# New order lists for the five engines of a four-layer graph network kernel, drawn up with two more costs counted

## The reference, cut to what matters

```python
x = _layernorm(x + _L0(x, adj))   # two hypergraph convolutions: H = (adj != 0), relu and a norm between them
x = _layernorm(x + _L1(x, adj))   # one softmax weight per node: softmax(q . (adj @ k)) times v
x = _layernorm(x + _L2(x, adj))   # attention, 8 heads of 32, scores times 2*adj, softmax, output projection
x = _layernorm(x + _L3(x, adj))   # gate from the degree, sigmoid scores times adj, divided by their sum, relu
```

## Time and profile before

| what | us |
|---|---|
| runs of the kernel, median (lowest to highest) | 962.69 (962.51 to 967.75) |
| profiled execution, span from first to last instruction | 966.0 |
| TensorE busy in the span | 887.1 (92%) |
| VectorE, ScalarE, GpSimd busy | 742.3, 724.6, 670.3 |
| steady part, from 194.1 to 857 | 662.9 |

### The profile page before, as it was taken

The page is one execution under the profiler, slowest core; times in us unless marked ns, Lnnn a source line. Parts: engine busy times, 40 slices in busy tenths (PEclk is TensorE's granted clock), DMA queues, the critical chain, the costliest instruction groups (busy, mean ns, idle before and its releaser), DMA issues.

```text
span 966.0 us, 34322 instructions
## 1 busy us (share of the span) xinstructions
PE 887.1 (92%) x12124; PEld 761.5 (79%) x12124; DVE 742.3 (77%) x2292; ACT 724.6 (75%) x1740; POOL 670.3 (69%) x1005
## 2 busy tenths in 40 slices
PE   4778898999999999999999999999999999988674
PEld 3556677888888888888888888888888888876542
DVE  5556776888888888888888888888888888876632
ACT  3445567888888888888888888888888888867631
POOL 2575667777777787777777777877778777764421
PEclk9798899999999999999999999999999999999955
DMA  8002443444454444444344444443443444444320
GB/s 207 20 21 83 111 100 65 119 111 106 112 123 121 116 116 102 103 112 109 106 109 110 122 123 117 114 106 99 111 119 103 104 115 116 109 97 116 97 48 22
DMA packets 194573, 99.46 MB, mean 103 GB/s; under 512 B 112866, under 2 KB 194276, under 8 KB 194532
## 3 DMA queue, kind: packets, MB, share of 16 engines
q1 hardware_dynamic: 194532, 98.93, 40.6%
HBM read 48.28 MB, written 25.17 MB: 76 GB/s over the span
## 4 chain that ended last, share of the span: by engine, by line
PE 53%; ACT 11%; POOL 10%; DVE 10%; issue 9%; DMA 5%; SPq 1%; POOLq 0%; DVEq 0%; ACTq 0%
PE bank L537 12%; PE bank L539 12%; PE bank L538 12%; POOL rFl L1375 3%; PE bank L562 3%; ACT r L886 3%; PE bank L754 2%; PE bank L815 2%; DMA k_by_head<-kst 2%; DMA Ks<-k_by_head 2%; PE bank L650 1%; ACT x L846 1%; PE bank L682 1%; ACT rFh L826 1%; POOL rsC L1391 1%
## 5 line engine op out<-in xcount | busy, mean ns | idle before, releaser
L1375 POOL TENSOR_TENSOR rFl<-r,rFh 128x512 f16<-128x512 f32 x64 | 74.2, 1160 | 81.1 <-ACT rFh L826 81.1
L537 PE MATMUL bank<-z1h,W 128*128 128x256 f16 x256 | 71.9, 281 | 6.3 <-DVE z1l L1025 6.3
L538 PE MATMUL bank<-z1l,W 128*128 128x256 f16 x256 | 71.8, 281 | 0.0
L537 PE MATMUL bank<-W,rFh 128*128 128x256 f16 x256 | 71.8, 280 | 0.0
L539 PE MATMUL bank<-z1h,W 128*128 128x256 f16 x256 | 71.7, 280 | 0.0
L539 PE MATMUL bank<-W,rFl 128*128 128x256 f16 x256 | 71.7, 280 | 0.0
L538 PE MATMUL bank<-W,rFh 128*128 128x256 f16 x256 | 71.7, 280 | 0.0
L1476 POOL TENSOR_TENSOR late<-late,Smx 128x512 f32<-128x512 f32 x64 | 66.8, 1043 | 1.3 <-DVE Smx L1282 1.0
L1375 POOL TENSOR_TENSOR y0l<-y,y0h 128x512 f16<-128x512 f32 x32 | 37.3, 1166 | 42.3 <-ACT y0h L826 42.3
L870 ACT ACTIVATE Pf<-bank,Dinv 128x128 f32<-128x128 f32 x64 | 20.0, 363 | 49.7 <-DVE Dinv L1167 49.7
L886 ACT ACTIVATE r<-bank,b1c 128x256 f32<-128x256 f32 x128 | 50.1, 471 | 4.8 <-PE bank L539 4.8
(11 more groups left out here) (281 smaller groups left out, 4188.3 us busy)
## 6 DMA issues: line engine op xcount, KB each, us to landing
Qs<-q_by_head SPq DMA_DIRECT2D x96, 128.0 KB, 2.7
Ks<-k_by_head SPq DMA_DIRECT2D x96, 128.0 KB, 3.2
Vbd<-vst SPq DMA_DIRECT2D x128, 66.0 KB, 2.1
xin<-x SPq DMA_DIRECT2D x32, 256.0 KB, 2.8
q_by_head<-qst SPq DMA_DIRECT2D x32, 256.0 KB, 2.5
k_by_head<-kst SPq DMA_DIRECT2D x32, 256.0 KB, 2.1
out<-late SPq DMA_DIRECT2D x32, 256.0 KB, 2.9
aC<-adj_mask SPq DMA_DIRECT2D x32, 65.0 KB, 2.2
```

The costliest lines, as they stand in the source:

```text
L537: pe.matmul(o, sh, mh, start=start, stop=False, skip_group_check=True)
L538: pe.matmul(o, sh, ml, start=False, stop=False, skip_group_check=True)
L1375: return pool.tensor_tensor(dst, a, b, ALU.subtract)
```

## The change

All lists of the five engines are replaced, apart from a few that come out the same; the pieces themselves, the waits and the buffers stay. The lists of before were drawn up in the same form; for the new ones two more costs are counted: what TensorE loses where the kind of matmul changes (part of the array or all of it), and that VectorE and GpSimd keep each other waiting at a port that they share. Two lines of the diff:

```diff
-ORDER_PE = [3, 2, 1, 5, 2, 4, 4, 2, 0, 3, 1, 0, 2, 0, 5, 4, 0, 0, 5, 3, 1, 3, 4, 5, 1, 2, 5, 5, 2, 0, 1, 0, 4]
+ORDER_PE = [3, 2, 1, 3, 2, 5, 0, 2, 1, 4, 4, 5, 0, 2, 0, 4, 1, 3, 3, 5, 0, 0, 5, 4, 1, 2, 5, 5, 1, 2, 0, 0, 4]
-ORDER_POOL = [0, 1, 0, 0, 1, 0, 3, 4, 1, 1, 1, 2, 1, 2, 0, 5, 3, 0, 0, 0, 4, 4, 3, 4, 5, 5, 5, 0, 0]
+ORDER_POOL = [1, 0, 0, 0, 1, 4, 0, 1, 1, 1, 3, 2, 1, 2, 5, 3, 0, 0, 0, 4, 4, 0, 3, 4, 5, 5, 5, 0, 0]
```

More of the change, by code:

```diff
@@ L61 @@
-TAIL_POOL = [[1, 1, 3, 4, 5, 1, 1, 1, 3, 1, 2, 2, 3, 4, 4, 4, 5, 5, 5], [4, 3, 5, 2, 2, 4, 4, 3, 3, 4, 5, 5, 5], [4, 5, 4, 4, 3, 4, 3, 5, 3, 5, 5], [4, 5, 4, 4, 4, 5, 5, 5], [5, 5, 5, 5]]
+ORDER_PE = [3, 2, 1, 3, 2, 5, 0, 2, 1, 4, 4, 5, 0, 2, 0, 4, 1, 3, 3, 5, 0, 0, 5, 4, 1, 2, 5, 5, 1, 2, 0, 0, 4]
+ORDER_SP = [3, 0, 3, 4, 3, 0, 0, 2, 3, 3, 5, 2, 2]
+HEAD_SP = [[0, 0, 0], [0, 0, 0], [0, 0, 2, 0, 2, 2], [3, 3, 3, 0, 0, 2, 3, 3, 0, 2, 2], [3, 3, 4, 0, 0, 3, 0, 2, 3, 3, 2, 2], [3, 4, 0, 3, 3, 0, 2, 3, 0, 3, 2, 2, 5]]
@@ new lines @@
+TAIL_SP = [[3, 4, 3, 3, 3, 5, 2, 3, 2, 2], [3, 3, 5, 3, 4, 3, 2, 3, 2, 2], [3, 4, 3, 3, 5, 3, 3], [5, 4], [5]]
+ORDER_ACT = [0, 3, 1, 4, 2, 3, 5, 0, 5, 0, 5, 1, 0, 2, 4, 4, 1, 4, 2, 0, 0, 5, 0, 0, 0, 0, 2, 1, 4, 3, 3, 4, 2, 3, 3, 4, 5]
+ORDER_DVE = [0, 0, 2, 0, 0, 2, 1, 0, 0, 3, 0, 3, 0, 0, 2, 1, 1, 4, 1, 4, 4, 2, 3, 4, 0, 5, 2, 5, 0, 3, 5, 5, 4, 1, 5, 3, 3, 5, 4, 2, 1, 5, 3, 5, 1, 1, 5, 2, 3, 3, 0, 0, 4, 0]
+ORDER_POOL = [1, 0, 0, 0, 1, 4, 0, 1, 1, 1, 3, 2, 1, 2, 5, 3, 0, 0, 0, 4, 4, 0, 3, 4, 5, 5, 5, 0, 0]
@@ new lines @@
+HEAD_PE = [[0, 0, 0, 0, 0, 6, 6, 6, 0, 0], [1, 0, 0, 0, 1, 0, 0, 1, 1, 0, 1, 0], [2, 1, 2, 0, 2, 0, 2, 0, 1, 0, 0, 2, 6, 1, 2, 1, 0, 1, 0], [3, 2, 1, 2, 3, 2, 1, 0, 2, 0, 3, 0, 3, 1, 0, 2, 0, 1, 2, 1, 0, 0], [1, 3, 2, 4, 4, 0, 3, 1, 0, 4, 2, 2, 0, 2, 4, 0, 3, 1, 0, 3, 2, 4, 1, 2, 1, 0, 0], [2, 1, 3, 5, 3, 2, 1, 0, 4, 4, 2, 5, 2, 0, 4, 5, 3, 0, 3, 4, 5, 0, 0, 1, 5, 2, 5, 1, 2, 1, 0, 0, 4]]
+HEAD_ACT = [[6, 0, 0, 0, 0, 0, 0, 0, 0, 0, 0, 6], [0, 6, 0, 0, 1, 0, 0, 0, 0, 1, 0, 0, 1, 0, 1], [6, 2, 0, 6, 0, 0, 1, 0, 2, 2, 0, 0, 2, 0, 1, 0, 0, 1, 0, 2, 1], [6, 6, 6, 6, 0, 3, 2, 6, 1, 3, 0, 0, 2, 1, 0, 1, 2, 3, 2, 0, 0, 0, 0, 0, 0, 2, 1, 6, 3, 3, 3], [4, 1, 3, 0, 0, 0, 2, 3, 4, 4, 0, 4, 1, 2, 4, 0, 2, 4, 0, 0, 1, 0, 0, 2, 0, 1, 4, 3, 2, 3, 3, 3], [0, 3, 1, 5, 5, 2, 4, 3, 5, 0, 0, 4, 2, 4, 0, 4, 2, 5, 1, 4, 0, 0, 0, 1, 0, 0, 2, 0, 3, 1, 3, 4, 2, 3, 3, 4, 5]]
@@ new lines @@
+HEAD_POOL = [[0, 0, 0, 6, 6, 0, 0, 0, 0, 0, 0, 0], [0, 0, 6, 0, 0, 1, 1, 1, 1, 1, 6, 1, 0, 0, 0, 0, 0, 0], [0, 0, 0, 0, 1, 1, 2, 2, 6, 1, 1, 1, 0, 0, 0, 0, 1, 0, 0], [0, 0, 1, 0, 0, 1, 3, 1, 1, 1, 2, 1, 3, 2, 3, 0, 0, 0, 0, 0, 0], [1, 0, 0, 0, 1, 3, 0, 4, 1, 1, 1, 1, 2, 2, 4, 4, 3, 4, 0, 0, 0, 0, 3, 0, 0], [1, 0, 1, 0, 0, 4, 3, 0, 1, 1, 2, 2, 5, 1, 3, 4, 1, 4, 0, 0, 0, 0, 3, 4, 5, 5, 5, 0, 0]]
+TAIL_PE = [[2, 1, 3, 5, 3, 2, 1, 2, 4, 4, 5, 2, 4, 5, 3, 3, 4, 5, 1, 2, 5, 5, 1, 2, 4, 1], [3, 3, 5, 4, 2, 4, 5, 4, 2, 2, 5, 2, 5, 3, 3, 4, 2, 5, 5, 2, 4], [3, 3, 5, 4, 4, 4, 5, 4, 5, 3, 3, 5, 5, 5, 4], [5, 4, 4, 5, 4, 5, 4, 5, 5, 5, 4], [5, 5, 5, 5, 5, 5]]
@@ new lines @@
+TAIL_ACT = [[3, 1, 2, 3, 5, 4, 5, 5, 4, 4, 2, 1, 2, 5, 4, 1, 2, 4, 3, 3, 4, 1, 3, 2, 3, 4, 5], [3, 4, 3, 5, 5, 5, 2, 4, 4, 4, 5, 2, 2, 3, 2, 4, 3, 4, 2, 3, 3, 4, 5], [3, 3, 5, 5, 4, 4, 4, 5, 4, 4, 5, 4, 3, 3, 3, 3, 4, 5], [5, 4, 5, 5, 4, 4, 4, 5, 4, 4, 4, 5], [5, 5, 5, 5, 5]]
+TAIL_DVE = [[2, 1, 3, 2, 1, 2, 1, 4, 2, 4, 3, 4, 5, 4, 3, 5, 1, 2, 5, 4, 5, 3, 5, 3, 3, 5, 3, 4, 1, 2, 5, 3, 5, 1, 5, 2, 3, 1, 4, 1], [3, 4, 2, 3, 4, 4, 4, 5, 2, 5, 2, 2, 5, 5, 5, 2, 3, 4, 5, 3, 3, 3, 4, 3, 2, 5, 3, 5, 5, 2, 3, 4], [3, 3, 4, 4, 4, 4, 4, 5, 3, 5, 4, 5, 5, 5, 3, 3, 5, 3, 3, 3, 5, 5, 3, 5, 4], [4, 4, 4, 4, 5, 5, 4, 5, 5, 5, 4, 5, 5, 5, 5, 4], [5, 5, 5, 5, 5, 5, 5, 5, 5]]
@@ L63 @@
+TAIL_POOL = [[1, 1, 3, 4, 1, 1, 1, 2, 2, 5, 1, 3, 3, 4, 4, 4, 5, 5, 5], [4, 3, 5, 2, 2, 3, 3, 4, 4, 4, 5, 5, 5], [3, 4, 5, 4, 4, 3, 3, 4, 5, 5, 5], [4, 5, 4, 4, 4, 5, 5, 5], [5, 5, 5, 5]]
 LAST_LAG = 5
```

9 lines of the change are left out of this document (1 added, 8 removed).

## The result

The changed kernel takes 971.03 us (median of 20 runs, 965.33 to 981.45), the kernel before 962.60 us in the same rounds: a ratio of 1.0089, 95% interval 1.0065 to 1.0113. It is slower by 0.9%, inside the band of 1% that was called the same and inside the range, and 7.6 us above the predicted 963.4.

What follows compares the result with a forecast made beforehand. TensorE was taken to bound the steady steps, chains of waits the head and tail. +0.20 us a step over 26 steps (+5.2) and -4.5 in the tail gave 963.4 us; range 955 to 972, over all cases 948 to 977.

Steps and rivals of the forecast that it cites:

- The turn of x1: Steady step: TensorE would newly wait about 0.7 us for normB in each step, bounds 0.2 and 0.9.
- Rival A: Faster: nbB misses Ql or VectorE's short ops are quicker, x1's turn waits only 0.2; -0.30 a step, 950.4 us; chance 0.27.
- Changes of kind: TensorE's steady step: ten changes between part and whole array become six, 0.35 us less a step, bounds 0.27 and 0.60.
- SAs: Steady step: TensorE's wait at the turn of SAs falls from 0.32 to some 0.15 us, 0.15 less a step.
- rival B: Slower: step's end becomes VectorE's, resb holds HBh, TensorE waits at L608 for HBl; +0.70 a step, 976.4 us; chance 0.23.
- the step's +0.20: Net steady-step forecast in us: -0.35 kinds, -0.15 SAs' wait, +0.70 x1's turn; 26 times, +5.2.
- the 26.6 to 26.8: Sign of a right forecast: steady steps of this length in us; below 26.3 or above 27 would show it wrong.
- SyncE: Keys' way through DRAM: starts earlier, covering the scores' moving forward; 0 taken, a failed cover joining the wait at x1's turn.
- the 0.7: The forecast wait in us of TensorE at the turn of x1 in each steady step.
- Tail: Context fills a gap in the last step but one, about 1.5 us earlier; three tail steps give -4.5, bounds 0 and 9.
- Head: No gain expected in the head: 0 us, bounds -4 and +4, a tenth of its idle time.

## Why the prediction was right, and where it was not

- **The turn of x1.** +0.70 forecast, 0.70 measured, on normB as said, with nbB beside Ql. That the size is met to the hundredth is luck: two terms were too large by 0.4 each. The turn came 3.2 nearer to L614, not 3.6, since conv2's wait and the turn of P's stand in front of it. The chain to normB's end became 1.0 shorter, not 1.4: from L614 to mvB's end are 3.30 where 3.1 was the most, preB starting only behind conv2, and the pair took 1.05 where 0.94 was put in. Rival A, whose point was that nbB misses Ql, fell with that.
- **Changes of kind.** -0.35 forecast, -0.25 measured: the term was mis-sized. o1 and uxT, which differ in rows only, cost 0.11 between them, twice what I kept for it. The rule of the Trainium skill's TensorEngine Tiling (Array Packing), section Tiling Modes, that every change of mode drains the engine, agrees with that row, and its sum (0.30) was the nearer one.
- **SAs.** -0.15 forecast, -0.21 measured.
- **What failed: rival B put in the wrong place.** I named its cause (GpSimd and VectorE late at the end of the step) but priced it only where it would hold HBh and TensorE would wait at L608, and set it aside because VectorE had 0.99 of cover there. So the sum has no term for it. The cover was used up: the low part of k, 0.87, moved into it, and y0 waits 0.30 for rsc. B's own meeting came as well, resb beside HBh, and HBh's two ops took 0.63 instead of 0.41; TensorE does not wait at L608 for it. What cost time came out at conv2, which waits 0.31 a step for y0l; the change had brought conv2 1.1 nearer to L608 (v's 1.34 out from between, the sum L696 in). And rvar was not the late one; the cause is the place of El0 and El1 beside veG and rsG, which I had read only as a delay for rvar, and which makes GpSimd reach y0l late. With it, and with 0.1 less for the kinds, the step's +0.20 becomes +0.6, 16.6 us where 5.2 stood: 27.12, and not the 26.6 to 26.8 that was to show the forecast right.
- **SyncE.** "If that cover fails, the wait joins the 0.7 rather than adding to it": the run with Ql moved shows that: the scores wait for Ks, 0.20 on the mean, once the turn hardly waits.
- **Tail.** -4.5 forecast, 5.7 in the profile. TensorE idles 3 to 4 us less in the tail; the rest goes with the clock. In the last step but one, the place that was priced, the context fills the gap (its second half waits 0.87 for its own input), the second projection no longer waits (the 0.93 of the earlier trace rows), and the turn of cx follows it at once:

```profile
932.67 0.87 PE L754 MATMUL bank<-Vbd,PT 128*64 128x66 f16 x24
934.41 0.57 PE L754 MATMUL bank<-Vbd,PT 128*64 128x66 f16 x24 [0.87 <-DMA PT<-Ehl]
934.92 0.28 PE L537 MATMUL bank<-Wl,xgFh 128*128 128x256 f16 x1
...
936.24 0.60 PE L562 MATMUL bank<-ident,late 128*128 128x128 f32 x4
937.81 0.22 PE L792 MATMUL bank<-Qh 128*64 128x64 f16 x2 [0.97 <-DVE y3l L1025]
```

  From the first projection to the turn of cx are 6.0 us instead of 9.2. TensorE idles 0.9 of them instead of 2.2, which is close to the forecast 1.5; the rest is the clock, 0.72 in this stretch instead of 0.50. Behind the turn s3 then waits 0.97 for y3l.

- **Head.** 0 forecast, with 4 as bound, and 5.1 came in the profile. But TensorE's idle time in the head is 40.2 us before, 39.8 and 40.2 in the two executions with the new ends and the old steady lists, and 38.1 in the changed kernel. So the waits gave 0 to 2, inside the bound, and the rest is busy time, at a clock of 0.94 to 0.95 instead of 0.92. Over the 13 profiles with these head lists the head ends between 160.9 and 166.6; of before there is one profile, with 167.3.
- **The sum.** By the profiles the steady steps missed by 9.5 us (14.7 where 5.2 stood), and the head by 5.1 and the tail by 1.2 the other way; these offset each other in part, and the forecast's place inside 1% owes something to that.

## What to carry to other kernels

In a list where several chains end together, shortening one of them alone gains little: each edit that moved one op out of the way of a wait in the changed step met another wait, of 0.2 to 0.8 us, within the same microsecond. So before moving an instruction read who waits for everything that it passes, not only for what it heads, and what else the op that it heads waits for: 0.69 us taken out in front of preB brought mvB forward by 0.01. When an order trades places, price a short op by its neighbour on the other engine: two subtractions of 0.7 us beside GpSimd's small ops cost 0.3 us in each step, more than the changes of kind saved. Time the head and tail lists apart from the steady ones, since one can hide the other's loss or gain, and compare TensorE's idle time there, not only the length, which moves with the clock of the execution.

## What the runs showed of the hardware that was not expected

- GpSimd's small ops lose by a meeting with VectorE too: veG of two numbers a partition takes 0.56 instead of 0.19 and rsG 1.03 instead of 0.71, in all 22 steps, when a subtraction of two SBUF tiles runs beside them, and both are back when it covers one head only.
- x2b on GpSimd met Ql in the run with vl behind aggrB and took 1.78 instead of 1.27; it had nobody waiting, and cost nothing.
- The times of one kernel can differ by 12 us: with the new ends and the steady lists of before the times ran from 952.0 to 964.0 (mean granted clock 0.979 in the first, 0.969 in the last). The two that were profiled, 952.0 and 956.2, both have a step of 26.48, and tails of 125.5 and 128.6 at a clock of 0.91 and 0.89. In the head the stretch from the fourth L608 to the fifth, with the same lists and 4.8 us of idle TensorE, took 22.9 us in seven profiles with a granted clock of 0.93 there, 27.8 and 27.9 in two with 0.75 and 0.76, and times between in the other four. The mean granted clock was 0.83 in the tail of before and 0.87 to 0.91 in the three with the new tail and old or new steady lists; the end of it decides, from 928 us on, before and in the changed kernel (windows as above):

```profile
928.00:966.00 38.00, 20.56 (x141) 12.50 (x140) 8.84 (x29) 8.96 (x20) 5.73 (x13) 0.54 0.04 14
```

```profile
928.00:969.90 41.90, 22.27 (x220) 14.93 (x220) 13.61 (x42) 13.28 (x29) 8.41 (x18) 0.73 0.12 31
```

The first is nearly all at the lower level (1.2 GHz), the second about half; TensorE is busy for little more than half of either stretch.
